# Two graph-attention layers on one core: a lighter feature, norm and score-offset path, and another order of steps on all five engines

## The chip, the cores and the metric

The kernel runs on one core of one Trainium2 chip. The metric is the device time of one execution in microseconds (us). TensorE is called PE below, VectorE DVE, ScalarE ACT, GpSimd POOL and SyncE SP; SP only issues DMAs here.

## What is computed

There are 64 graphs of 128 nodes with 384 features. Each passes a dot-product attention layer with 6 heads, a residual and a layer norm, then an additive attention layer with 12 heads, an elu, a sigmoid gate and a second layer norm. All of it is float32.

```python
q, k, v = heads(x @ Wq + bq), heads(x @ Wk + bk), heads(x @ Wv + bv)
probs = softmax(q @ k.T / sqrt(64) + where(adj, 0, -9e15))
x = layernorm(x + (probs @ v) @ Wf + bf)
h = einsum('bnd,ade->bane', x, W);  th = tanh(h)
attn = leaky_relu(th @ w_src + swap(th @ w_dst), 0.2)
attn = softmax(where(adj, attn, -999))
feat = elu(attn @ h + b)
gate = sigmoid(x @ H_w.T + H_b)
x = layernorm(x + gate * feat + (1 - gate) * x)
```

## The kernel before

Work goes by pairs of graphs (g is 0 or 1 in a pair), 32 pairs in all. The kernel is a software pipeline: in turn t of the loop, stage 0 handles the first layer of pair t, stage 1 the projections and scores of the second layer of pair t-1, and stage 2 the second attention product and the output of pair t-2. Stage -1 loads the next pair. A step called with `turn.late(s, ...)` in an engine's turn t belongs to the turn before, so it handles pair t-1-s, and a step called with `turn.step(s, ...)` handles pair t-s. Every engine runs its own list of steps strictly in the order written at the end of its block, and waits on semaphores (`now(...)`, `prev(...)`) for what other engines make. The lists of the five engines need not turn over at the same moment: an engine may be in its turn t+1 while PE is in turn t.

float32 products are made from rounded parts. A linear product takes three matmul passes (`product`, high and low parts), so ACT writes the high part of each operand and DVE the low part. The values `v` and the features `h` are cut in three bfloat16 parts: ACT writes parts 1 and 2, POOL makes the residue (`value_residue`, `hidden_residue`) and part 3 (`value_part3`, `hidden_part3`). `attend0(g)` on PE waits for `v_done[2][g]`, which is `value_part3(g)` on POOL.

For one pair the path around the change is this. `source_target_transposes` (line 502) turns the small score parts of the second layer, ACT copies them (`source_target_copy`, line 762), and `targets_flat` on SP issues six small DMAs (line 398) that lay them out in rows, which `attention1(g)` (lines 586 and 590) reads. The adjacency of a pair is loaded twice: `load_adj0` (line 381) for the first layer, where POOL makes `mask0` from it (`mask0_bias`, line 1238) for `scores(g)`, and `load_adj1` (line 387) for the second. `load_transposed_x` (line 369) brings the next pair's transposed input, from which ACT makes `xt_hi` (`next_x_high`). On SP the order before is:

```python
turn.late(0, load_adj1)
turn.late(-1, load_x)
turn.step(-1, load_transposed_x)
turn.step(1, targets_flat)
turn.step(-1, load_adj0)
turn.late(2, store, 0)
turn.late(2, store, 1)
```

On POOL, `mask0_bias` of pair t stands behind `value_residue(0)` of the same pair, and `value_part3(1)` of pair t comes in the same turn. PSUM banks are shared by rotation: `TP_USERS` and `LIN_USERS` name the users in PE's order, and the next user of a bank waits for the last reader of the one before.

Of the kernel before, what the change touches and what calls it, by code (L numbers as in the profile page):

```python
# [17 lines left out]
H0 = 6  # L18
E0 = D // H0
H1 = 12  # L20
# [3 lines left out]
MASKED = 9e15 / SCALE0  # L24
# [78 lines left out]
def turns(eng, passed, body, prepare=None):  # L103
# [10 lines left out]
    for t in range(PAIRS - 1, PAIRS + 3):  # L114
# [5 lines left out]
TP_USERS = ("ct1", "wt00", "wt01", "wt02", "x1t0", "wt10", "x1t1", "wt11", "wt12", "pt01", "sdt", "pt00",  # L120
             "pt11", "pt10", "ct0")
# [4 lines left out]
LATE_USERS = ("g1", "z1", "ct1", "pr0", "pr1")  # L126
# [19 lines left out]
def two_layer_graph_attention(nc, x, x_t, adj, weights, biases, row_biases, out):  # L146
    with ExitStack() as ctx:
# [20 lines left out]
        half_neg = sb("half_neg", [128, 1])  # L168

# [19 lines left out]
        p0_max = sb("p0_max", [128, 2, H0])  # L189
        p0_shift = sb("p0_shift", [128, 2, H0])  # L190
# [57 lines left out]
        bv_ready = signal("bv_ready", 0, 1)  # L248
        bv_mm = signal("bv_mm", 0, 1)
        bias_row_loaded = signal("bias_row_loaded", 0, 1)  # L250
        bias_split = signal("bias_split", 0, 1)
        bias_loaded = signal("bias_loaded", 0, 1)
# [17 lines left out]
        sc_mm, sc_max = pair_of("sc_mm", 0), pair_of("sc_max", 0)  # L270
        sc_shift, sc_exp = pair_of("sc_shift", 0), pair_of("sc_exp", 0)
# [29 lines left out]
        f_bias, f_min, f_exp = pair_of("f_bias", 2), pair_of("f_min", 2), pair_of("f_exp", 2)  # L301
# [41 lines left out]
        def _(sp):  # L343
# [18 lines left out]
            def body(turn):  # L362
# [58 lines left out]
        def _(pe):  # L421
# [16 lines left out]
            def body(turn):  # L438
# [180 lines left out]

                turn.late(1, gate_rows, 1)  # L620
# [7 lines left out]
                turn.step(0, queries_keys, 1)  # L628
                turn.step(2, attend1, 0, 0)
                turn.step(2, weights1_transposes, 0, 2)  # L630
                turn.step(0, values, 0)
                turn.step(2, attend1, 0, 1)
                turn.step(1, x1_transposes, 0)
                turn.step(0, queries_keys, 2)
                turn.step(2, attend1, 0, 2)
                turn.step(1, hidden, 0)
                turn.step(2, weights1_transposes, 1, 0)
# [18 lines left out]
                turn.step(0, context_transposes, 0)  # L656
# [6 lines left out]
        def _(act):  # L663
            def weight_high(n):
                act.wait_ge(w_loaded[n].sem, 16)
                act.activation(w_hi[n][:, :, :].rearrange("p c d -> p (c d)"), staging[n], ACT.Copy)\
                    .then_inc(w_hi_ready[n].sem, 1)
# [5 lines left out]
            def other_weights():  # L673
                act.wait_ge(small_loaded.sem, 16 * SMALL)

                act.activation(x1t_hi[:, 0, :, :], column["bv"][:, :].unsqueeze(2).to_broadcast([128, C, N]),
                               ACT.Copy).then_inc(bv_ready.sem, 1)
                for n in ("Wf", "W1", "Hw"):
                    weight_high(n)
# [7 lines left out]
            def body(turn):  # L687
# [18 lines left out]
                def keep_x1(g):  # L706
                    act.wait_ge(x1_ready[g].sem, prev(x1_ready[g]))

                    act.wait_ge(y2_ready[g].sem, now(y2_ready[g]))
                    act.activation(x1_kept[:, g, :], x1[:, g, :], ACT.Copy).then_inc(x1_copied[g].sem, 1)  # L710
# [7 lines left out]
                def hidden_part1(g):  # L718

                    act.wait_ge(f_mm[g].sem, now(f_mm[g]))  # L720
                    act.activation(h_part[0][:, g, :, 0:E1],
                                   lin_bank(f"h{g}")[:, 0:D].rearrange("p (a e) -> p a e", a=H1),
                                   ACT.Copy).then_inc(h_done[0][g].sem, 1)

                def hidden_copy(g):
                    act.wait_ge(h_mm[g].sem, now(h_mm[g]))

                    act.wait_ge(h_done[2][g].sem, prev(h_done[2][g]))
                    act.activation(h_res[:, g, :], lin_bank(f"h{g}")[:, 0:D], ACT.Copy).then_inc(h_raw[g].sem, 1)
# [49 lines left out]
                def scores_exp(g):  # L779
                    act.wait_ge(sc_shift[g].sem, now(sc_shift[g]))  # L780
# [3 lines left out]
                    for h in range(H0):  # L784
                        last = act.activation(p0[:, g, N * h:N * (h + 1)], zp[:, h // C, N * (h % C):N * (h % C + 1)],  # L785
                                              ACT.Exp, bias=p0_shift[:, g, h:h + 1], scale=SCALE0)
# [39 lines left out]

                def elu_exp(g):
# [581 lines left out]
```

## Time and profile before

| | |
|---|---|
| median of 3 runs | 1347.98 us (1346.89 to 1348.66) |
| the profiled execution, its own time | 1350.65 us |
| its span, first to last instruction | 1348.9 us |
| PE busy | 1200.5 us, 89% |
| DVE busy | 1077.4 us, 80% |
| POOL busy | 1006.0 us, 75% |
| ACT busy | 990.9 us, 73% |

The span is compared with the profiled execution's own time; the median of other executions is 2.67 us below that. Matmuls overlap, so a busy share of PE counts a little more than its rate; idle time is the surer sign.

### The profile page before, as it was taken

Reading aid. Unit: us, or ns where it says so; the run is one execution under the profiler, and the core shown is the slowest. Engines: PE = TensorE matmul, PEld = TensorE weight load, DVE = VectorE, ACT = ScalarE, POOL = GpSimd, SP = SyncE. Lnnn points to the kernel's source line nnn. Section 1 sums busy time; section 2 is a strip of 40 time slices with the busy share of each in tenths; the row PEclk is TensorE's granted clock in tenths of the full one; section 3 lists DMA queues with packets and bytes.
Section 4 is the critical chain, followed back from the end, with each engine's and each line's share of the span. In section 5 each row is a group of like instructions: output and inputs, shape, how many; then the busy total and the mean of one; then the engine's idle time right before and its main releaser. Section 6 shows DMA issues by size and latency. Waiting matters only on the chain.

```text
span 1348.9 us, 37937 instructions
## 1 busy us (share of the span) xinstructions
PE 1200.5 (89%) x13193; PEld 1066.4 (79%) x13193; DVE 1077.4 (80%) x2138; ACT 990.9 (73%) x2058; POOL 1006.0 (75%) x941
## 2 busy tenths in 40 slices
PE   4899999999999999999999999999999999999963
PEld 4788788888878888878888887888887888887752
DVE  5478788888888888888888888888888888888864
ACT  4377777777777777777777777777778778777753
POOL 1257877778887777887777788777788777878766
PEclk9799999999999999999999999999999999999976
DMA  3100010111010111101011100011110101110000
GB/s 130 50 27 28 16 39 25 37 37 37 14 37 24 37 37 38 37 14 37 24 37 37 37 19 33 25 36 37 37 37 14 37 24 37 37 37 26 15 13 24
DMA packets 46172, 44.86 MB, mean 33 GB/s; under 512 B 24757, under 2 KB 41146, under 8 KB 46138
## 3 DMA queue, kind: packets, MB, share of 16 engines
q1 hardware_dynamic: 46138, 44.42, 10.1%
q8 instruction: 20, 0.33, 0.1%
q14 instruction: 14, 0.11, 0.0%
HBM read 31.22 MB, written 12.58 MB: 32 GB/s over the span
## 4 chain that ended last, share of the span: by engine, by line
PE 53%; POOL 13%; issue 12%; DVE 10%; ACT 9%; DMA 1%; SPq 0%; DVEq 0%; POOLq 0%; ACTq 0%
PE lin L427 31%; PE tp L600 5%; DVE z L1084 4%; ACT p L785 3%; POOL f L1306 3%; PE zp L528 2%; POOL y L1331 2%; PE tp L565 2%; POOL v_res L1274 2%; PE zp L586 2%; PE fp L612 2%; POOL v_part L1278 2%; PE fp L553 2%; PE zp L590 2%; POOL rstd L1295 1%
## 5 line engine op out<-in xcount | busy, mean ns | idle before, releaser
L1300 POOL TENSOR_TENSOR z<-z,z_max 128x1536 f32<-128x1536 f32 x64 | 176.3, 2755 | 18.0 <-DVE z_max L1091 18.0
L1291 POOL TENSOR_TENSOR rstd<-rstd,half_neg 128x1 f32<-128x1 f32 x64 | 35.2, 549 | 163.3 <-DVE rstd L1071 163.3
L1253 POOL TENSOR_TENSOR prod<-th,w_sd_rows 128x768 f32<-128x768 f32 x64 | 120.1, 1876 | 36.0 <-ACT th L716 36.0
L824 ACT ACTIVATE p1t_hi<-tp 128x512 f16<-128x512 f32 x192 | 110.6, 593 | 37.6 <-PE tp L600 37.6
L1099 DVE SCALAR_TENSOR_TENSOR p1t_lo<-tp,p1t_hi 128x512 f16<-128x512 f32 x192 | 129.4, 688 | 8.0 <-ACT p1t_hi L824 5.0
L612 PE MATMUL fp<-h_part,p1t_hi 128*128 128x33 bf16 x2304 | 115.6, 179 | 4.5 <-DVE p1t_lo L1099 4.4
L612 PEld LDWEIGHTS fp<-h_part,p1t_hi 128*128 128x128 f16 x2304 | 102.5, 97 | 18.4 <-issue 12.7
L600 PE MATMUL tp<-ident,z 128*128 128x128 f32 x768 | 109.5, 280 | 7.4 <-ACT z L819 5.9
L1084 DVE SCALAR_TENSOR_TENSOR z<-zp,z 128x1536 f32<-128x1536 f32 x64 | 111.8, 1748 | 3.2 <-ACT z L794 3.2
L1091 DVE TENSOR_REDUCE z_max<-z 128x12 f32<-128x1536 f32 x64 | 111.3, 1738 | 0.1
L785 ACT ACTIVATE p<-zp,p_shift 128x128 f32<-128x128 f32 x384 | 105.6, 382 | 5.9 <-DVE p_shift L1022 5.9
L615 PE MATMUL fp<-h_part,p1t_lo 128*128 128x33 bf16 x1536 | 109.6, 178 | 0.0
L819 ACT ACTIVATE z<-z 128x1536 f32<-128x1536 f32 x64 | 95.3, 1488 | 13.8 <-POOL z L1300 13.8
L427 PE MATMUL lin<-xt_hi,Wq_hi 128*128 128x256 f32 x288 | 86.6, 301 | 18.4 <-POOL xt_lo L1283 18.0
L600 PEld LDWEIGHTS tp<-ident,z 128*128 128x128 f32 x768 | 90.5, 144 | 10.9 <-ACT z L819 6.7
L794 ACT ACTIVATE z<-zp 128x1536 f32<-128x1536 f32 x64 | 92.9, 1451 | 2.1 <-PE zp L590 2.1
L615 PEld LDWEIGHTS fp<-h_part,p1t_lo 128*128 128x128 f16 x1536 | 93.2, 96 | 0.0
L1331 POOL TENSOR_TENSOR y<-f,x_kept 128x384 f32<-128x384 f32 x64 | 64.8, 1013 | 34.7 <-ACT out_tile L835 29.6
L1313 POOL TENSOR_SCALAR f_neg<-f 128x384 f32<-128x384 f32 x64 | 74.8, 1168 | 12.8 <-POOL f L1306 11.9
L427 PE MATMUL lin<-xt_lo,Wq_hi 128*128 128x256 f32 x288 | 81.3, 282 | 0.0
L427 PE MATMUL lin<-xt_hi,Wq_lo 128*128 128x256 f32 x288 | 81.1, 282 | 0.0
L427 PE MATMUL lin<-xt_hi,Wk_hi 128*128 128x256 f32 x288 | 80.9, 281 | 0.0
(163 smaller groups left out, 4805.3 us busy)
## 6 DMA issues: line engine op xcount, KB each, us to landing
xt_raw<-x_t SPq DMA_DIRECT2D x32, 384.0 KB, 3.6
x_raw<-x SPq DMA_DIRECT2D x32, 384.0 KB, 3.1
out<-out_tile SPq DMA_DIRECT2D x64, 192.0 KB, 1.9
dst_row<-sd_t SPq DMA_DIRECT2D x192, 3.0 KB
adj<-adj SPq DMA_DIRECT2D x64, 32.0 KB, 1.9
z<-Wq SPq DMA_DIRECT2D x1, 576.0 KB, 3.6
z<-Wk SPq DMA_DIRECT2D x1, 576.0 KB, 4.6
p<-Wv SPq DMA_DIRECT2D x1, 576.0 KB, 6.6
```

What stands on the lines that cost most here:

```text
L427: last = pe.matmul(bank, a(k), b(k), start=(opens and k == 0 and i == 0), stop=(k == C - 1 and i == 2))
L600: last = pe.transpose(bank[:, N * i:N * (i + 1)], z[:, g, c:c + N], ident[:, :])
L612: pe.matmul(o, hi, h_part[i][:, g, h, :], start=(h == 0 and i == 0), stop=False, skip_group_check=True)
L615: last = pe.matmul(o, lo, h_part[i][:, g, h, :], start=False, stop=(i == 1), skip_group_check=True)
L785: last = act.activation(p0[:, g, N * h:N * (h + 1)], zp[:, h // C, N * (h % C):N * (h % C + 1)], ACT.Exp, bias=p0_shift[:, g, h:h + 1], sc ...
L819: act.activation(z[:, g, :], z[:, g, :], ACT.Exp).then_inc(z_exp[g].sem, 1)
L824: act.activation(p1t_hi[:, g, 4 * N * k:4 * N * (k + 1)], tp_bank(f"wt{g}{k}")[:, :], ACT.Copy, scale=PSCALE).then_inc(wt_hi[k][g].sem, 1)
L1084: dve.scalar_tensor_tensor(out=z[:, g, :], in0=zp[:, :, :].rearrange("p b n -> p (b n)"), scalar=0.2, in1=z[:, g, :], op0=ALU.mult, op1=AL ...
L1091: dve.tensor_reduce(z_max[:, g, :], z[:, g, :].rearrange("p (a n) -> p a n", a=H1), AX.X, ALU.max).then_inc(z_maxed[g].sem, 1)
L1099: dve.scalar_tensor_tensor(out=p1t_lo[:, g, c], in0=bank[:, :], scalar=PSCALE, in1=p1t_hi[:, g, c], op0=ALU.mult, op1=ALU.subtract)\
L1253: pool.tensor_tensor(prod[:, g, :].rearrange("p (s d) -> p s d", s=2), th[:, g:g + 1, :].to_broadcast([128, 2, D]), rows["w_sd"][:, :].rea ...
L1300: pool.tensor_tensor(zs, zs, z_max[:, g, :].unsqueeze(2).to_broadcast([128, H1, N]), ALU.subtract)\
```

## The change

Five things are altered.

- Features: b1 is added to the features `h` before they are cut in parts, on DVE while it copies them out of PSUM (`hidden_raised`, in place of ACT's `hidden_copy`). The stored b1 is raised by 1, so the attention output arrives as f+1. POOL's `features_bias` and its minimum are gone; ACT computes relu(1-(f+1)) and then exp of its negative, and DVE takes a plain maximum. `x1_kept` is also raised by 1, which cancels in the difference.
- Norms: the shift of each layer norm is a `tensor_scalar` with one tensor input instead of a `scalar_tensor_tensor` with two.
- Score offset: Wq and bq carry the factor and a minus sign, so DVE's minimum serves directly as the bias of the exponential and `scores_shift` is gone.
- The four small steps on the score parts handle both graphs in one instruction each instead of one per graph.
- The order of steps is another on PE, ACT, DVE, POOL and SP, with the bank rotation to match.

```diff
-TP_USERS = ("ct1", "wt00", ..., "pt11", "pt10", "ct0")
+TP_USERS = ("ct0", "ct1", "wt00", ..., "pt11", "pt10")
...
 # SP
-                turn.late(0, load_adj1)
-                turn.late(-1, load_x)
-                turn.step(-1, load_transposed_x)
+                turn.late(2, store, 0)
                 turn.step(1, targets_flat)
                 turn.step(-1, load_adj0)
-                turn.late(2, store, 0)
+                turn.step(-1, load_transposed_x)
+                turn.step(0, load_adj1)
                 turn.late(2, store, 1)
+                turn.late(-1, load_x)
...
 # PE
+                turn.late(0, context_transposes, 0)
                 turn.late(1, gate_rows, 1)
                 turn.late(1, attention1, 1)
                 turn.late(0, context_transposes, 1)
...
                 turn.step(1, attention1, 0)
-                turn.step(0, context_transposes, 0)
                 turn.step(0, attend0, 1)
...
 # ACT
+                def features_negative(g):
+                    act.wait_ge(f_norm[g].sem, now(f_norm[g]))
+                    act.wait_ge(f_elu[g].sem, prev(f_elu[g]))
+                    act.activation(f_neg[:, g, :], f[:, g, :], ACT.Relu, bias=one[:, :], scale=-1.0)\
+                        .then_inc(f_min[g].sem, 1)
...
                 turn.step(1, gate_tanh, 0)
                 turn.step(1, z_copy, 0)
                 turn.step(-1, next_x_high)
-                turn.step(1, hidden_part2, 0)
-                turn.step(1, hidden_part2, 1)
                 turn.step(0, context_high, 0)
-                turn.step(1, gate_quarter, 0)
-                turn.step(1, keep_x1, 0)
+                turn.late(2, norm1, 1)
+                turn.step(1, gate_tanh, 1)
+                turn.step(0, context_high, 1)
...
 # DVE
+                def hidden_raised(g):
+                    dve.wait_ge(h_tanh[g].sem, now(h_tanh[g]))
+                    dve.wait_ge(h_done[2][g].sem, prev(h_done[2][g]))
+                    dve.tensor_tensor(h_res[:, g, :].rearrange("p (a e) -> p a e", a=H1),
+                                      lin_bank(f"h{g}")[:, 0:D].rearrange("p (a e) -> p a e", a=H1),
+                                      rows["b1"][:, :].unsqueeze(1).to_broadcast([128, H1, E1]), ALU.add)\
+                        .then_inc(h_raw[g].sem, 1)
...
-                    dve.scalar_tensor_tensor(out=shift0[:, g, :], in0=moments[:, g, 0:1], scalar=-1.0,
-                                             in1=rstd[:, g, :], op0=ALU.mult, op1=ALU.mult)\
+                    dve.tensor_scalar(shift0[:, g, :], moments[:, g, 0:1], rstd[:, g, :], -1.0, ALU.mult, ALU.mult)\
...
+                turn.late(0, weights0_low, 1, 1)
+                turn.late(2, variance1, 0)
+                turn.late(2, elu, 1)
                 turn.late(0, context_inverse, 1)
-                turn.late(2, variance1, 0)
+                turn.late(1, z_leak, 0)
                 turn.late(0, context_norm, 1)
-                turn.late(1, z_leak, 0)
...
 # POOL: the whole new order
+                turn.late(1, hidden_residue, 0)
+                turn.late(2, gated_features, 0)
+                turn.late(0, value_part3, 0)
+                turn.late(2, mix, 0)
+                turn.late(0, value_residue, 1)
+                turn.step(0, mask0_bias)
+                turn.late(0, value_part3, 1)
+                turn.late(1, hidden_residue, 1)
+                turn.late(2, deviation1, 0)
+                turn.late(2, features_difference, 1)
+                turn.late(2, gated_features, 1)
+                turn.late(-1, next_x_low)
+                turn.late(1, z_subtract, 0)
+                turn.step(1, mask1_bias)
+                turn.late(2, mix, 1)
+                turn.late(1, hidden_part3, 0)
+                turn.late(0, deviation0, 0)
+                turn.late(1, z_subtract, 1)
+                turn.late(0, deviation0, 1)
+                turn.late(1, hidden_part3, 1)
+                turn.step(0, value_residue, 0)
+                turn.step(1, source_target_products, 0)
+                turn.step(1, source_target_products, 1)
+                turn.late(2, deviation1, 1)
+                turn.step(2, features_difference, 0)
```

## Rows read from the trace of the kernel before

**Rows 1.** Stretches: busy time of each engine and count, granted clock, DMA, one steady turn.
```profile
core 0: us, PE busy (x) PEld busy (x) DVE busy (x) ACT busy (x) POOL busy (x), PEclk, DMA share, GB/s
...
600.00:640.00 40.00, 37.10 (x416) 33.09 (x415) 33.27 (x68) 30.76 (x66) 31.63 (x30) 1.00 0.10 32
```

**Rows 2.** Who waited for whom: us in total, times, longest us.
```profile
PE tp L565 <- DVE p0t_lo L1030: 38.6, 30, 1.4
```

**Rows 3.** Timeline of PE: start us, us, what, idle before it and its releaser.
```profile
630.36 0.28 PE L502 MATMUL tp<-ident_bf,sd_parts 128*128 128x128 bf16 x2 [0.42 <-DVE sd_parts L990]
...
632.98 0.25 PE L553 MATMUL fp<-v_part,p0t_hi 128*128 128x65 bf16 x3 [0.27 <-POOL v_part L1278]
...
635.54 0.81 PE L590 MATMUL zp<-dst_row,sd_t 128*128 128x512 bf16 x3
637.71 0.52 PE L565 MATMUL tp<-ident,ctx_n 128*128 128x128 f32 x3 [1.35 <-DVE p0t_lo L1030]
638.17 0.25 PE L553 MATMUL fp<-v_part,p0t_hi 128*128 128x65 bf16 x3
...
641.78 0.39 PE L586 MATMUL zp<-mask,ident_bf 128*128 128x512 bf16 x1 [0.76 <-DVE z L1084]
...
670.12 0.28 PE L502 MATMUL tp<-ident_bf,sd_parts 128*128 128x128 bf16 x2 [0.41 <-DVE sd_parts L990]
```

**Rows 4.** Timeline of SP, the same turn.
```profile
631.59 4.74 SPq L398 DMA_DIRECT2D dst_row<-sd_t  x6
636.61 0.39 SPq L381 DMA_DIRECT2D adj<-adj  x1
637.37 0.98 SPq L405 DMA_DIRECT2D out<-out_tile  x2
```

**Rows 5.** Line 381, the load of the adjacency.
```profile
DMA to landing us min/median/max: 1.7/1.8/6.8
```

**Rows 6.** Timeline of POOL, the same turn.
```profile
619.04 0.40 POOL L1238 TENSOR_SCALAR mask<-adj 128x256 bf16<-128x256 uint8 x1
619.52 1.01 POOL L1306 TENSOR_TENSOR f<-f,b_rows 128x384 f32<-128x384 f32 x1
...
631.99 0.89 POOL L1278 TENSOR_TENSOR v_part<-v_res,v_part 128x384 bf16<-128x384 f32 x1
```

**Rows 7.** Groups of the page: the instructions that the feature edit removes or resembles.
```profile
L1313 POOL TENSOR_SCALAR f_neg<-f 128x384 f32<-128x384 f32 x64 | 74.8, 1168 | 12.8 <-POOL f L1306 11.9
L1306 POOL TENSOR_TENSOR f<-f,b_rows 128x384 f32<-128x384 f32 x64 | 64.3, 1005 | 7.9 <-DVE f L1112 5.5
L829 ACT ACTIVATE f_neg<-f_neg 128x384 f32<-128x384 f32 x64 | 34.3, 536 | 39.2 <-POOL f_neg L1313 39.2
```

**Rows 8.** Lines 1078 and 1134: ns min/median/max, first and last start.
```profile
L1078 DVE SCALAR_TENSOR_TENSOR shift<-moments,rstd x64: 95/598/2230, 61.0 to 1293.5; 128x1 f32<-128x1 f32 x64
...
L1134 DVE TENSOR_SCALAR rstd<-moments x64: 113/144/155, 122.6 to 1344.4; 128x1 f32<-128x1 f32 x64
```

**Rows 9.** Timeline of PE where its granted clock is low, and after.
```profile
1287.24 0.25 PE L612 MATMUL fp<-h_part,p1t_hi 128*128 128x33 bf16 x3 [1.90 <-DVE p1t_lo L1099]
...
1307.48 0.36 PE L502 MATMUL tp<-ident_bf,sd_parts 128*128 128x128 bf16 x2 [3.41 <-DVE sd_parts L990]
1307.63 0.53 PE L471 MATMUL lin<-bias_rows,ones_bf 128*128 128x384 bf16 x1
...
1310.52 0.52 PE L427 MATMUL lin<-Hw_hi,x1t_lo 128*128 128x384 f32 x1
...
1312.79 0.34 PE L471 MATMUL lin<-bias_rows,ones_bf 128*128 128x384 bf16 x1 [0.22 <-ACT gate L770]
...
1314.36 0.34 PE L427 MATMUL lin<-Hw_hi,x1t_lo 128*128 128x384 f32 x1
```

**Rows 10.** Stretches with low clock (columns as in rows 1).
```profile
1287.50:1297.00 9.50, 7.07 (x76) 6.33 (x73) 5.71 (x13) 3.85 (x6) 6.40 (x6) 0.50 0.01 2
...
1307.70:1310.90 3.20, 3.20 (x13) 2.89 (x11) 0.95 (x4) 0.91 (x2) 2.85 (x4) 0.50 0.02 5
```

More of the change, by code:

```diff
@@ L635, in body @@
                 turn.step(2, attend1, 0, 2)
+                turn.step(2, weights1_transposes, 1, 0)
                 turn.step(1, hidden, 0)
-                turn.step(2, weights1_transposes, 1, 0)
                 turn.step(1, x1_transposes, 1)
@@ L876, in body @@
                 turn.step(0, scores_exp, 0)
+                turn.step(1, hidden_part1, 0)
                 turn.step(0, value_part1, 1)
+                turn.step(0, weights0_high, 0, 1)
                 turn.step(0, value_copy, 1)
-                turn.step(0, weights0_high, 0, 1)
                 turn.step(1, hidden_part1, 1)
-                turn.step(1, hidden_copy, 1)
                 turn.late(2, norm1, 0)
@@ L884, in body @@
                 turn.step(0, weights0_high, 0, 0)
+                turn.step(0, scores_exp, 1)
+                turn.step(2, features_negative, 1)
                 turn.step(0, value_part2, 1)
-                turn.step(0, scores_exp, 1)
-                turn.step(2, elu_exp, 1)
                 turn.step(0, weights0_high, 1, 1)
                 turn.step(0, weights0_high, 1, 0)
-                turn.late(2, norm1, 1)
+                turn.step(2, elu_exp, 1)
                 turn.step(1, gate_tanh, 0)
@@ L1158, in body @@
                 turn.late(0, variance0, 0)
+                turn.late(2, stats1, 1)
                 turn.step(2, weights1_low, 0, 0)
[L1160 removed]
                 turn.step(2, weights1_low, 0, 1)
                 turn.late(0, shift_norm0, 0)
+                turn.step(0, queries_keys, 0)
+                turn.late(0, stats0, 1)
+                turn.late(2, moments1, 1)
                 turn.step(0, queries_keys, 1)
[L1164 to L1166 removed]
                 turn.late(0, moments0, 1)
@@ L1170, in body @@
                 turn.step(1, x1_low, 0)
-                turn.late(2, variance1, 1)
-                turn.step(2, features_inverse, 0)
-                turn.late(0, shift_norm0, 1)
-                turn.step(2, features_norm, 0)
-                turn.step(0, queries_keys, 2)
-                turn.step(1, x1_low, 1)
+                turn.late(0, shift_norm0, 1)
+                turn.step(2, features_inverse, 0)
+                turn.step(0, queries_keys, 2)
+                turn.step(2, features_norm, 0)
+                turn.step(1, x1_low, 1)
+                turn.late(2, variance1, 1)
                 turn.step(2, weights1_low, 1, 0)
-                turn.step(0, scores_max, 0)
+                turn.step(0, scores_min, 0)
+                turn.step(1, hidden_raised, 0)
                 turn.step(2, elu, 0)
-                turn.step(0, scores_shift, 0)
                 turn.step(1, source_target_sums, 0)
```

175 lines of the change are left out of this document (68 added, 107 removed).

## The prediction

> **What bounds the kernel now.** I read the stretches first. In a steady stretch of 40 us PE is busy 37.10, DVE 33.27, POOL 31.63, ACT 30.76 [rows 1]. PE is the bound, and what is left to gain lies in its waits. The timeline of PE gives the length of a turn: the small transposes of line 502 start at 630.36 and again at 670.12, so a turn lasts 39.76 us [rows 3]. In this turn PE waits 0.42 us for the score parts, 0.27 for POOL's third value part, 1.35 for DVE's `p0t_lo` ahead of the context transposes of line 565, and 0.76 for `z` [rows 3]; a further 0.3 or so lies in overlaps lost at these points. The list of waits confirms that the third is a steady one: 30 times, 38.6 us in all [rows 2]. If every wait went, a turn would be near 37, the busy time. That is the most that a new order can give: about 2.8 us a turn, 85 to 90 us in all.
>
> **The lighter work.** POOL loses line 1306 (1.005 us) and line 1313 (1.168 us), twice a turn: 4.35 us of 31.6 [rows 7]. ACT gains a relu twice a turn; the trace has none, the nearest row is the exponential of the same shape, 0.536 us [rows 7], and it loses as many copies of that size (`hidden_copy`): about zero, between -0.5 and +0.5 us a turn. DVE gains `hidden_raised` (two additions of about the size of a 128x384 operation, some 0.55 us each), and loses `scores_shift` and half of the small score instructions. Its norm offsets are the interesting part: the two-input form of line 1078 has a median of 598 ns and up to 2230 for one element a partition, while the one-input form of line 1134 on the same shape never takes more than 155 [rows 8]. If the new offsets behave like line 1134, the first of them alone saves DVE around 0.45 us twice a turn by the medians; at worst they stay as they are, nothing. All of this shortens engines that are not the bound. I cost it at nothing in the steady turn, because PE's remaining work covers it: DVE and POOL have 6 to 8 us of slack a turn. Where that cover is absent, in the drain after the last pair has left PE's dense part, the feature path is shorter by 1.005 + 1.168 - 0.536 = 1.64 us per graph; with two graphs partly overlapped, and less queueing on POOL, I take 4 us, from bounds 0 and 8.
>
> **The new order, step by step.** On PE, `context_transposes(0)` leaves its place ahead of `attend0(1)` and goes behind it, so `attend0(1)` now stands directly behind `attention1(0)`. With DVE's `weights0_low` and ACT's `weights0_high` brought forward, that takes away most of the 1.35 us wait, if `attend0(1)` gets its other input in time. That input is `value_part3(1)` from POOL, and here I find the trouble. It must be followed through three queues.
>
> POOL's turn t+1 now begins with the late steps of turn t, and in their middle stands `turn.step(0, mask0_bias)`. As a `step` it belongs to pair t+1. Behind it in the queue is `late value_part3(1)`, of pair t, which PE wants for `attend0(1)` in its turn t. `mask0_bias` waits for the adjacency of pair t+1. SP issues that load in its turn t, behind `targets_flat`, and `targets_flat` waits for the score copy of PE's turn t, that is, for line 502 near the turn's end. Before, SP had the same order of these two, but POOL asked for the mask early in the next turn, at 619.04 against a load issued at 636.61 less one turn, 596.9, and nothing waited [rows 4, 6]. Now a chain closes inside one turn:
>
> - from line 502 on PE to the first flat DMA: 631.59 - 630.36 = 1.23 us [rows 3, 4];
> - the six issues on SP: 4.74 us [rows 4];
> - to the issue of `load_adj0`: 636.61 - 636.33 = 0.28 us [rows 4];
> - its landing: 1.8 us, least 1.7 [rows 5];
> - `mask0_bias` to the next instruction of POOL: 619.52 - 619.04 = 0.48 us [rows 6];
> - `value_part3(1)` and the hand-over to PE: 632.98 - 631.99 = 0.99 us [rows 3, 6].
>
> The sum is 9.5 us from line 502 to the start of `attend0(1)`. Before, it was 638.17 - 630.36 = 7.81 us [rows 3].
>
> The rest of the turn, from `attend0(1)` to the next line 502, was 39.76 - 7.81 = 31.95 us. Out of it I take both waits in it, 0.76 and 0.42, since the new orders bring `z_leak` and the score parts forward and the stall in front gives DVE and ACT time to catch up; the moved transposes come in, 638.17 - 637.71 = 0.46. That is 31.23 us. The new turn is 31.2 + 9.5 = 40.8 us after rounding up a little for hand-overs, 1.0 longer than before. If one of the two waits stays it is 41.5.
>
> Who stands behind the stalled instruction: on POOL `value_part3(1)`, `hidden_residue(1)`, the features of graph 1 and `next_x_low`; on PE everything. The moves on SP make two more loads late. `load_transposed_x` now follows `load_adj0`, and ACT's `next_x_high` waits for it with `context_high(0)`, `norm1(1)` and `gate_tanh(1)` behind it; and `load_x` goes behind a store that waits for that `norm1(1)`. By the same rows both arrive 1 to 7 us after `attend0(1)` starts, about when PE's own steps need them. I cost these at nothing, at most 0.5 us a turn; their cover is the stall itself.
>
> **The clock.** The stall is long for PE. In the chain, the last matmuls ahead of it (line 590) start 5.18 us after line 502 at the distance of before (635.54 - 630.36) and run 0.81 [rows 3], so PE then stands idle 9.5 - 6.0 = 3.5 us each turn. Where PE had stood idle 3.41 us, its clock was granted at 0.50 from then on (1.2 GHz) for some 3 us, and after 1.90 us idle near 1287 it stayed there for the 9.5 us shown [rows 9, 10]; the waits of 1.35 us in the steady turns leave it at 1.00 [rows 1, 3]. So I expect the low level after most stalls. Its price: the ten matmuls of a gate product take 1310.52 - 1307.63 = 2.89 us between first and last start at the low level and 1314.36 - 1312.79 = 1.57 at the high one [rows 9], so 46% of low time is lost. For a stretch of 3.2 us, as in the second row [rows 10], that is 1.5 us; for one of 9.5 us, 4.4; and 0 if the clock holds. I take 1.5, as PE's work is dense behind this stall, like behind the one of 3.41 us. The Trainium skill (TensorE: Matmul & The Clock Gate, section The HAM clock gate) says that an idle stretch puts the engine back to half its clock and that sustained work releases it; by that rule the turn is 42.3 us, and if 3.5 us idle were still short enough for it, 40.8. By that rule, the trace agrees: it fell after 3.41 us idle.
>
> **Sum.** The load of pair t+1 exists for t up to 30, and `targets_flat` has work from turn 1, so 30 turns carry the chain: 30 x (1.0 + 1.5) = 75 us. Turn 31 has no next mask and keeps the good of the new order, -3; the drain -4; the first two turns, whose line 502 to `attend0(1)` was shorter than later, +1. From the profiled execution: 1350.65 + 75 - 6 = 1419.7. The median of the runs lies 2.67 below it: 1417.
>
> **Rivals.**
>
> The order works (other side). If the mask's input were there when POOL comes to it, `attend0(1)` would start about 5.4 us after line 502 (7.81 less 1.35, 0.46, 0.27 and some lost overlap), and a turn would cost PE's own work, about 37 us: 32 x 2.8 = 90 less, and 4 in the drain: 1254. It decides at one point: the chain from line 502 to the end of `mask0_bias` would have to take under 4.4 us, and the six issues alone take 4.74 [rows 4]. For it speak the idle list of PE and the lighter POOL. 0.12, mostly for an error of mine in the turn to which a step belongs.
>
> The chain holds but the clock doesn't fall: 30 x 1.0 - 6 = +24, 1372. The stall would be interrupted or shortened, for instance by line 590 itself waiting for its DMAs. 0.2.
>
> The chain, and long low stretches: 30 x (1.0 + 4.4) - 6 = +156, 1504. Against it speaks the dense work behind the stall. 0.1.
>
> The edits cancel: the six issues turn out shorter, or more of the old waits goes than I counted, and a turn stays at 39.8: 1344 with the drain's gain. 0.06.
>
> **Numbers.** My forecast, chain and one low stretch a turn, has 0.52. Its own range is 1390 to 1455, from 0.7 to 1.9 us for clock and old waits around the 2.5. The 8-in-10 range takes in the rival without a clock drop and leaves out the two far ones: 1363 to 1460. A measurement of this kernel tells about 0.2% from no change. Slower by more than that: 0.52 + 0.2 + 0.1 and a part of the wash, 0.84; faster 0.13; the same 0.03.
>
> **What would show it.** In the profile after: PE's largest idle before line 553 of `attend0(1)`, released by POOL's `v_part`, near 3.5 us a turn; on POOL an idle gap before `mask`, ended by the DMA of `adj`; a turn of 42.3 us between two starts of line 502, 9.5 of it to `attend0(1)`; granted clock near 0.95 on average in steady turns instead of 1.00; the wait of line 565 for `p0t_lo` gone; the norm offsets at some 150 ns. Wrong would be: a turn of 37 us with no wait for the mask (then I have misread the queues), or the stall there with the clock at 1.00 (then only the last term falls).

## The result and the profile after

The changed kernel takes 1461.35 us (median of four executions) against 1348.32 us (1346.89 to 1348.87) for the kernel before: 1.083 times as long, interval 1.0807 to 1.0854. Three of the four took 1457.42 to 1461.69 us; the fourth took 1940.06 us in a slow state, at a mean granted clock of 0.557, and is left out of the ratio. The profiled execution has an own time of 1461.69 us, a span of 1460.0 us and a mean granted clock of 0.921. The sign and the chain behind it were forecast, 1417 us was 44 us too low, and the time lies 1.35 us above the top of the range.

A long stretch of steady turns of the changed kernel (columns as in [rows 1]):

```profile
600.00:1000.00 400.00, 354.82 (x3762) 320.52 (x3760) 285.01 (x567) 280.07 (x589) 240.63 (x226) 0.93 0.10 28
```

PE is busy 35.5 us in 40 here, 37.1 before [rows 1], although part of the 35.5 runs at half clock and is thereby longer. The clock is 0.93 where it was 1.00. No engine has become the bound; PE waits. The list of waits over the whole span (us in total, times, longest) says for what:

```profile
POOL mask L1243 <- DMA adj<-adj: 178.2, 27, 6.8
...
PE fp L553 <- POOL v_part L1283: 110.8, 30, 4.3
ACT xt_hi L849 <- DMA xt_raw<-x_t: 77.8, 30, 3.3
```

The first two lines are the forecast chain: POOL waits for an adjacency that wasn't waited for before, and PE for the value part queued behind that mask. The wait of line 565 for `p0t_lo` [rows 2] is gone. One turn on PE, the counterpart of [rows 3] (in other turns the wait of line 553 is up to 4.3 us, 3.7 on average):

```profile
643.09 0.28 PE L502 MATMUL tp<-ident_bf,sd_parts 128*128 128x128 bf16 x2 [0.87 <-DVE sd_parts L1004]
643.64 0.52 PE L538 MATMUL tp<-ident,p 128*128 128x128 f32 x3 [0.27 <-DVE p0t_lo L1038]
...
647.99 0.81 PE L590 MATMUL zp<-dst_row,sd_t 128*128 128x512 bf16 x3
652.91 0.33 PE L553 MATMUL fp<-v_part,p0t_hi 128*128 128x65 bf16 x3 [4.12 <-POOL v_part L1283]
...
658.42 0.95 PE L586 MATMUL zp<-mask,ident_bf 128*128 128x512 bf16 x3
```

From line 502 to `attend0(1)` it is 652.91 - 643.09 = 9.82 us (forecast: 9.5). Line 586 no longer waits for `z` (0.76 before). But line 502 still waits for the score parts, and longer: 0.87 us where [rows 3] had 0.42. Line 502 starts at 74.9 the first time and at 1422.2 the last, 31 turns apart, so the mean turn is 1347.3 / 31 = 43.46 us; worked out in the same way it was 1230.6 / 31 = 39.70 before. All "mean turns" below are of this kind. The last of the 31 is short, 35.1 us, since no next pair is loaded in it; the 30 that carry the chain take 43.74 on average, against 39.65 before. Of these 30, 25 take 43.2 to 44.4 us and 5 take 41.4 to 42.7. One of each kind, columns as in [rows 1]:

```profile
643.09:687.34 44.25, 38.99 (x412) 35.25 (x413) 31.30 (x63) 30.62 (x64) 26.65 (x26) 0.92 0.10 29
731.57:774.31 42.74, 37.63 (x412) 34.12 (x413) 31.31 (x63) 30.68 (x64) 26.65 (x26) 0.96 0.11 30
```

The work is the same; the granted clock is 0.92 in the 25 longer turns and 0.96 in the 5 shorter ones, so the low level lasts about twice as long in most turns as in the few short ones.

The chain on SP and POOL, against [rows 4, 6]:

```profile
644.22 4.67 SPq L398 DMA_DIRECT2D dst_row<-sd_t  x6
649.36 0.39 SPq L381 DMA_DIRECT2D adj<-adj  x1
650.05 0.35 SPq L369 DMA_DIRECT2D xt_raw<-x_t  x1
```

```profile
643.88 0.89 POOL L1279 TENSOR_TENSOR v_res<-v_res,v_part 128x384 f32<-128x384 f32 x1
651.44 0.40 POOL L1243 TENSOR_SCALAR mask<-adj 128x256 bf16<-128x256 uint8 x1 [6.67 <-DMA adj<-adj]
651.93 0.89 POOL L1283 TENSOR_TENSOR v_part<-v_res,v_part 128x384 bf16<-128x384 f32 x1
```

Line 381 is issued 6.27 us after line 502 starts; the mask starts 2.08 us later and `v_part` 0.49 after that; 0.98 us more and PE goes on. Two stretches behind the stall show the price in clock:

```profile
653.00:660.00 7.00, 7.00 (x51) 5.89 (x51) 4.44 (x5) 2.42 (x4) 5.64 (x6) 0.59 0.27 82
660.00:666.00 6.00, 6.00 (x44) 5.83 (x42) 4.28 (x6) 4.49 (x6) 4.33 (x4) 1.00 0.01 2
```

PE is busy without a gap from 653 to 660, at a granted clock of 0.59 on average, that is, mostly at the lower of its two levels, 1.2 GHz.

The norm offsets became cheap, though not as cheap as the 150 ns of the forecast: line 1086 takes 204 ns in the median (202 to 214), where the old form took 598 and up to 2230 [rows 8].

The growing wait at line 502 needs VectorE and GpSimd side by side. The four steps that make the score parts, on DVE in the changed kernel:

```profile
640.03 0.33 DVE L991 CAST sd_parts<-sd 128x48 bf16<-128x48 f32 x1 [0.20 <-DVE sd L982]
...
640.87 0.36 DVE L995 TENSOR_TENSOR sd_res<-sd,sd_parts 128x48 f32<-128x48 f32 x1
641.33 0.84 DVE L1000 CAST sd_parts<-sd_res 128x48 bf16<-128x48 f32 x1
642.27 0.76 DVE L1004 TENSOR_TENSOR sd_parts<-sd_res,sd_parts 128x48 bf16<-128x48 f32 x1
```

and GpSimd at the same time:

```profile
640.28 0.88 POOL L1267 TENSOR_TENSOR h_res<-h_res,h_part 128x384 f32<-128x384 f32 x1
641.12 1.00 POOL L1316 TENSOR_TENSOR f<-f,gate 128x384 f32<-128x384 f32 x1
642.09 0.88 POOL L1283 TENSOR_TENSOR v_part<-v_res,v_part 128x384 bf16<-128x384 f32 x1
```

The last three small operations end at 641.23, 642.17 and 643.03, and the GpSimd operations at 641.16, 642.12 and 642.97: each within 0.07 us behind the other. The kernel before, in the same place of a turn, on DVE:

```profile
667.97 1.07 DVE L978 TENSOR_TENSOR sd_res<-sd,sd_parts 128x24 f32<-128x24 f32 x2
669.07 0.26 DVE L984 CAST sd_parts<-sd_res 128x24 bf16<-128x24 f32 x2
...
669.80 0.26 DVE L990 TENSOR_TENSOR sd_parts<-sd_res,sd_parts 128x24 bf16<-128x24 f32 x2
```

and on POOL:

```profile
667.91 1.00 POOL L1323 TENSOR_TENSOR f<-f,gate 128x384 f32<-128x384 f32 x1
669.89 1.03 POOL L1331 TENSOR_TENSOR y<-f,x_kept 128x384 f32<-128x384 f32 x1 [0.99 <-ACT out_tile L835]
```

There the pair of line 978, started under a GpSimd operation, took 1.07 us, and the pair of line 984, in GpSimd's gap, 0.26. It looks as if a small operation sits on DVE until GpSimd's is over. That is so far a reading; e6 below tests it.

### The profile page after: what moved, and what is told of

It is laid out like the page before. It is cut to its first block, busy times and chain, and to the rows that moved or that the text cites. A ratio compares the mean times of both kernels' runs of the same rounds, so it can differ in the third digit from the quotient of the medians.

```text
span 1460.0 us, 37822 instructions
## 1 busy us (share of the span) xinstructions
PE 1257.6 (86%) x13193; PEld 1133.9 (78%) x13193; DVE 1022.5 (70%) x2011; ACT 994.6 (68%) x2060; POOL 856.1 (59%) x813
## 4 chain that ended last, share of the span: by engine, by line
issue 26%; PE 22%; POOL 21%; DVE 14%; SPq 9%; DMA 4%; ACT 2%; POOLq 0%; DVEq 0%; ACTq 0%
PE lin L427 11%; SPq L398 8%; POOL prod L1258 8%; POOL z L1305 5%; DMA adj<-adj 3%; PE fp L553 2%; DVE z L1091 2%; PE tp L565 2%; POOL rstd L1296 2%; DVE sd L982 2%; POOL v_res L1279 2%; DVE y L1066 2%; POOL v_part L1283 2%; DVE sd_parts L1000 2%; PE zp L586 2%
## 5 line engine op out<-in xcount | busy, mean ns | idle before, releaser
L553 PE MATMUL fp<-v_part,p0t_hi 128*128 128x65 bf16 x1152 | 82.6, 213 | 113.5 <-POOL v_part L1283 110.8
L553 PEld LDWEIGHTS fp<-v_part,p0t_hi 128*128 128x128 f16 x1152 | 70.6, 110 | 133.7 <-issue 133.7
L1045 DVE RECIPROCAL ctx_rcp<-fp 128x6 f32<-128x6 f32 x64 | 12.5, 196 | 180.7 <-PE fp L556 180.7
L1243 POOL TENSOR_SCALAR mask<-adj 128x256 bf16<-128x256 uint8 x32 | 13.4, 417 | 214.3 <-DMA adj<-adj 178.2
L1106 DVE SCALAR_TENSOR_TENSOR p1t_lo<-tp,p1t_hi 128x512 f16<-128x512 f32 x192 | 126.0, 683 | 3.6 <-ACT p1t_hi L821 3.5
L612 PE MATMUL fp<-h_part,p1t_hi 128*128 128x33 bf16 x2304 | 111.6, 178 | 1.2 <-DVE p1t_lo L1106 1.2
L782 ACT ACTIVATE p<-zp,p_min 128x128 f32<-128x128 f32 x384 | 105.9, 388 | 5.6 <-DVE p_min L1030 5.6
L1296 POOL TENSOR_TENSOR rstd<-rstd,half_neg 128x1 f32<-128x1 f32 x64 | 35.1, 549 | 117.1 <-DVE rstd L1079 117.1
L427 PE MATMUL lin<-Hw_hi,x1t_hi 128*128 128x384 f32 x192 | 95.6, 498 | 0.0
```

What stands on the lines that cost most here:

```text
L427: last = pe.matmul(bank, a(k), b(k), start=(opens and k == 0 and i == 0), stop=(k == C - 1 and i == 2))
L553: pe.matmul(o, hi, v_part[i][:, g, head, :], start=(h == 0 and i == 0), stop=False, skip_group_check=True)
L612: pe.matmul(o, hi, h_part[i][:, g, h, :], start=(h == 0 and i == 0), stop=False, skip_group_check=True)
L1106: dve.scalar_tensor_tensor(out=p1t_lo[:, g, c], in0=bank[:, :], scalar=PSCALE, in1=p1t_hi[:, g, c], op0=ALU.mult, op1=ALU.subtract)\
```

## The experiments

All times below are medians, of two executions in e2, e3 and e5 and of four to ten in the others; each ratio is to the kernel before as measured beside that run (1348.37 to 1349.39 us). Unless something else is said, each kernel is the changed one with the edit shown.

**e1, the adjacency ahead of the targets' copies.**

```
 turn.late(2, store, 0)
+turn.step(-1, load_adj0)
 turn.step(1, targets_flat)
-turn.step(-1, load_adj0)
```

> The changed kernel with one step moved on SP: load_adj0 ahead of targets_flat. Theory (the mask's load behind the six flat issues holds POOL's third value part, and PE with it): the wait of line 553 for POOL's v_part goes, and with it the low clock. The transposed input still loads behind the flat issues, about 9.7 us after line 502, so ACT's xt_hi waits and with it the context's high part; PE would wait some 1.5 us for that. A turn of 38 to 39.5 us instead of 44.25, in all 1265 to 1310 us. Rival (the new order of PE, ACT and DVE is itself worse, and the mask only one of several waits): a turn stays above 42 us, over 1390 us.

1356.33 us, 1.0049 of before (1.0023 to 1.0076), mean turn 40.11. The edit of one line gives back 105 of the 113 us, so the loss hangs on the chain through SP. POOL no longer waits for the adjacency beyond 0.5 us and PE's 4.12 us are 0.28. The level was missed by 46 us, since two loads are still late:

```profile
DVE y L1066 <- DMA x_raw<-x: 52.0, 27, 2.3
...
ACT xt_hi L849 <- DMA xt_raw<-x_t: 50.8, 30, 2.6
```

and PE now feels it:

```profile
653.64 0.35 PE L427 MATMUL lin<-xt_hi,Wq_hi 128*128 128x256 f32 x1 [0.77 <-DVE y L1066]
```

**e2, adjacency and transposed x ahead of the targets' copies.**

```
 turn.late(2, store, 0)
+turn.step(-1, load_adj0)
+turn.step(-1, load_transposed_x)
 turn.step(1, targets_flat)
-turn.step(-1, load_adj0)
-turn.step(-1, load_transposed_x)
```

> The changed kernel with load_adj0 and load_transposed_x both ahead of targets_flat on SP. Theory: nothing of stage -1 is late any more; a turn of 36.8 to 38 us, near PE's own work, in all 1230 to 1275 us, and 20 to 50 us less than with load_adj0 alone. Rival (the transposed input's lateness costs nothing, as the prediction had it): the same time as with load_adj0 alone, within 10 us.

1309.91 us, 0.9703 of before (0.9672 to 0.9734): mean turn 38.63, 46 us below e1, inside the 20 to 50 expected, and faster than the kernel before, but 35 us above the level expected. What was left:

```profile
693.49 0.28 PE L502 MATMUL tp<-ident_bf,sd_parts 128*128 128x128 bf16 x2 [0.88 <-DVE sd_parts L1004]
```

```profile
655.40:661.40 6.00, 5.49 (x58) 4.10 (x59) 4.39 (x12) 5.19 (x15) 3.83 (x5) 1.00 0.37 106
...
694.70:697.90 3.20, 3.20 (x22) 2.89 (x21) 1.19 (x4) 2.85 (x9) 1.13 (x3) 0.52 0.45 131
```

The same wait at line 502 as in the changed kernel is there in every turn (655.42, 693.49, 733.12). Behind the one at 655.42 the clock stays at 1.00 and the turn takes 38.07 us; behind the one at 693.49 it is 0.52 for 3.2 us and the turn takes 39.63. Each time PE waits 0.88 us and, at line 538, 0.27 us more; behind it the clock falls in 8 of the 28 turns that have these two waits, each time for 1.5 us more, and in the other 20 it doesn't.

**e3, the mask behind the last value part on POOL**, SP's order left as in the changed kernel.

```
+turn.late(0, value_part3, 1)
 turn.step(0, mask0_bias)
-turn.late(0, value_part3, 1)
```

> The changed kernel, SP's order untouched, with mask0_bias and late value_part3(1) swapped on POOL, so that the third value part no longer stands behind the mask. Theory: attend0(1) starts some 5 to 6 us after line 502 instead of 9.8 and the clock stays up; POOL still idles for the mask until some 8.5 us after line 502, so next_x_low and the features behind it are late, and PE waits 1 to 3 us for xt_lo or xt_hi instead: a turn of 38.5 to 41 us, in all 1280 to 1360 us. Rival (what holds PE is that POOL as a whole is late, whatever stands behind the mask): the turn stays within 1 us of 44.25.

1380.78 us, 1.0228 (1.0184 to 1.0272), mean turn 40.82: the turn is inside the 38.5 to 41 expected, the time 21 us above the 1360 expected at most. The chain can be cut on POOL as well as on SP: PE waits 0.28 us at `attend0(1)`, released by DVE. The loads stay late, ACT's copy of x_t waits 86.4 us in all (77.8 before this edit), and PE waits 0.85 us for `y` and 0.66 for `ctx_lo`. So it is worth 24 us less than e1. The clock stays up as expected: it falls in 1 of the 28 turns in which PE, here too, waits 0.89 us at line 502 and 0.27 at line 538.

**e4, the kernel before with the changed kernel's order of SP's steps**, and nothing else.

```
-turn.late(0, load_adj1)
-turn.late(-1, load_x)
-turn.step(-1, load_transposed_x)
+turn.late(2, store, 0)
 turn.step(1, targets_flat)
 turn.step(-1, load_adj0)
-turn.late(2, store, 0)
+turn.step(-1, load_transposed_x)
+turn.step(0, load_adj1)
 turn.late(2, store, 1)
+turn.late(-1, load_x)
```

> The kernel before with only the changed kernel's order of SP's steps (store, targets, first adjacency, transposed x, second adjacency, store, x); every other engine keeps its order. My theory: the order of SP's loads costs what it does only together with GpSimd's new place for the mask, ahead of the last value part; in the old GpSimd order the mask reads an adjacency that was loaded some 20 us earlier. The transposed x is now issued about 28 us later, right behind the adjacency (676.8 in the turn at 671), and lands some 3.4 us after, while ScalarE copied it at 678.7: up to 1.8 us of wait on ScalarE in a turn, most of it absorbed. Expected 1345 to 1385 us, no wait of TensorE on the value parts. Rival: SP's order is harmful by itself, whatever GpSimd does: 1420 us or more.

1360.26 us, 1.0087 (1.0064 to 1.011). SP's order costs 11 us by itself (ACT stands idle for 1.21 us ahead of its copy of x_t in a turn) and not 113: the loss needs both, loads behind the copies and the mask ahead of the value part.

**e5, PE kept busy in the stall.** Sixteen matmuls of 128x512 more a turn ahead of `attend0(1)`, whose results nothing reads:

```
+if g == 1:
+    for _ in range(16):
+        pe.matmul(fp[:, 0:512], ones_bf, ident_bf (repeated), start=True, stop=True)
 pe.wait_ge(v_done[2][g].sem, now(v_done[2][g]))
```

> The changed kernel, with 16 extra matmuls of 512 columns whose result is overwritten, placed on PE in the stall ahead of the wait for POOL's v_part in attend0(1), so that PE has work while it stalls. The stall itself stays. Theory (the low clock after the stall costs 2.3 us a turn): the granted clock stays at 1.00 in the steady turns and a turn falls from 44.25 to about 41.9 us, in all 1385 to 1400 us. Rival (the slower matmuls lie beside other waits and cost little): the clock stays up and the time falls by less than 20 us.

1409.45 us, 1.044 (1.0404 to 1.0476), mean turn 41.75:

```profile
600.00:1000.00 400.00, 384.89 (x4127) 335.31 (x4126) 299.34 (x600) 295.21 (x622) 255.69 (x239) 0.99 0.10 29
```

More work on PE, and 52 us less time. The chain is as it was, POOL waits 178.3 us for the adjacency against 178.2, and the clock is at 0.99. The low clock therefore costs at least 52 us of the changed kernel's time, (43.46 - 41.75) = 1.7 us a turn. That is less than the 2.3 us that I expected, and the time is 9 us above the 1400 expected at most. It is a lower bound for two reasons: 8 of the first 30 turns are still at 0.96, and the last turn, which has no stall for the sixteen matmuls to fill, went from 35.1 to 39.6 us. The 22 turns at a clock of 1.00 take 41.58 us on average, against the 43.74 of the changed kernel: about 2.2 us a turn that carries the chain.

**e6, e2 with GpSimd idle while the score parts are made.** A wait more on POOL, behind the two products:

```
+def hold():
+    pool.wait_ge(sd_3.sem, now(sd_3))
 ...
 turn.late(2, deviation1, 1)
+turn.step(1, hold)
 turn.step(2, features_difference, 0)
```

> The kernel with the first adjacency and the transposed x ahead of the targets (1309.91 us), and GpSimd now waits, behind the two products, until VectorE has written the third score part. There VectorE's four small operations took 0.33, 0.36, 0.84 and 0.76 us, each of the last three ending within 0.06 us of the end of a GpSimd operation; TensorE waited 0.88 us at L502 in every turn, and in every second turn a stretch of half clock followed (turns of 38.1 and 39.6 us). Theory: VectorE's operations that read two tensors or a tensor in SBUF are held by a running GpSimd operation; with GpSimd idle each takes under 0.25 us, the wait at L502 is under 0.2 us, the low stretches behind it go too, and the turn is 37.2 to 37.6 us: 1255 to 1280 us. Rival: the small operations are slow because they are merged (48 elements in three dimensions), so the wait at L502 stays at 0.7 us or more: 1305 us or more, longer still for GpSimd's lost time. Second rival: the wait goes, and GpSimd's 2 us later value parts make TensorE wait at the context product instead: 1290 to 1330 us.

1301.06 us, 0.9636 (0.9617 to 0.9655); mean turn 38.34. Line 502 doesn't wait any more in the steady turns (3.0 us in two waits at the start, 32.0 in 32 waits in e2), and 29 of the first 30 turns are at a clock of 1.00. The four operations, still merged and with nothing of them changed, take 0.19 to 0.21 us each with GpSimd idle, the last two a quarter of their time (shown from e12, which has the same wait):

```profile
640.87 0.19 DVE L991 CAST sd_parts<-sd 128x48 bf16<-128x48 f32 x1 [0.20 <-DVE sd L982]
...
641.61 0.20 DVE L995 TENSOR_TENSOR sd_res<-sd,sd_parts 128x48 f32<-128x48 f32 x1
641.91 0.19 DVE L1000 CAST sd_parts<-sd_res 128x48 bf16<-128x48 f32 x1
642.20 0.21 DVE L1004 TENSOR_TENSOR sd_parts<-sd_res,sd_parts 128x48 bf16<-128x48 f32 x1
```

The merging is thereby excluded as the cause, and it is shown that these operations are held while GpSimd works. But the time fell by 9 us and not by 30 to 55; the second rival is what came: GpSimd's 2.5 us are missing further on.

```profile
651.56 0.25 PE L553 MATMUL fp<-v_part,p0t_hi 128*128 128x65 bf16 x3 [1.12 <-POOL v_part L1283]
```

**e7, the changed kernel's operations in the old orders.** All lighter operations, every engine's steps and PSUM banks as before.

```
 turn.step(0, scores_min, 0)
+turn.step(1, hidden_raised, 0)
 ...
+turn.step(2, features_negative, 0)
 turn.step(2, elu_exp, 0)
```

> The changed kernel's operations (one addition less and no minimum on GpSimd, relu on ScalarE, the bias added to the hidden values on VectorE, minimum of negative scores, merged score parts, new offsets) in the old order on every engine and with the old banks; only the steps that are new stand beside their neighbours (the relu ahead of the exponential, the raised values behind the minimum of the scores and behind the shift of the second norm). Theory: the lighter work lies off the path that sets the turn, so the time is that of the kernel before within 15 us: 1333 to 1363 us, and all of the loss of 113 us is the order's. Rival: the lighter work is what would have paid and gives 20 us or more by itself: 1325 us or less. Second rival: the operations themselves cost, since VectorE has an addition of 0.55 us more for each graph where ScalarE had a copy: 1370 us or more.

1344.45 us, 0.9966 (0.9957 to 0.9976). The lighter work is worth 4.6 us, about what the forecast gave to the drain, and all of the loss is the order's. The first 30 turns take 39.69 us on average, 39.65 before. This kernel also settles where the growth at line 502 comes from: with the merged operations in the old order PE waits 17.8 us there in all (18.3 before, 31.8 in the changed kernel), and the last two of them take 0.19 and 0.20 us, both started in a gap of 1.02 us in GpSimd's work.

**e8, the kernel before with e6's wait.**

```
 turn.step(1, source_target_products, 1)
+turn.step(1, hold)
```

> The kernel before with one wait more: GpSimd waits behind the two products until VectorE has written the third score part. VectorE's residues there took 1.07 us for two while a GpSimd operation ran, and its other small operations 0.13 us each. Theory: TensorE's wait of 0.42 us at L502 goes or nearly goes, and GpSimd, which was idle for 1.0 us in that stretch anyway, is 1 to 2 us later with the minimum that ScalarE's exponential waits for: 1335 to 1365 us. Rival: the later minimum holds ScalarE's copies of the weights behind it, which TensorE waits for at the context product: 1365 us or more.

1413.42 us, 1.0477 (1.0458 to 1.0496): far worse, and my theory wrong, the rival right in size but with another place. In the old order POOL makes graph 0's last value part behind the gated features, the mask and the mix, all of which the wait delays; PE then stands still at `attend0(0)`, for which the profile names no releaser:

```profile
655.03 0.28 PE L502 MATMUL tp<-ident_bf,sd_parts 128*128 128x128 bf16 x2
660.15 0.25 PE L553 MATMUL fp<-v_part,p0t_hi 128*128 128x65 bf16 x3 [2.78 <-issue]
```

POOL writes that part at 659.17 for 0.88 us, and PE goes on at 660.15. 0.42 us were removed at line 502 and 2.78 put in 5 us later. The clock was 0.97 in the steady stretch.

**e9, e6 with graph 0's last value part between the two products.**

```
 turn.step(1, source_target_products, 0)
+turn.step(0, value_part3, 0)
 turn.step(1, source_target_products, 1)
 ...
-turn.late(0, value_part3, 0)
```

> The kernel in which GpSimd waits for the third score part (1301.06 us; turn 38.45), with one step moved: GpSimd writes graph 0's last value part (0.9 us) between the two products, where it waits 1.0 us for the second tanh, instead of behind the gated features. In the run with the wait alone, L502 no longer waited, and TensorE waited 1.12 us for that part ahead of the context product of graph 0. Theory: that wait was all that took the gain; it goes, 0.3 to 0.5 us at the context product of graph 1 stay, no low stretches of the clock: turn 37.2 to 37.6, 1255 to 1275 us. Rival: the part in the new place delays the second product and with it the score parts, so that L502 waits again: 1290 us or more.

1294.96 us, 0.9587 (0.956 to 0.9614), mean turn 38.13. Neither case came: no wait at line 502 nor at either `attend0`, and yet 6 us only, since the next input in line is the targets' copies:

```profile
651.35 0.59 PE L590 MATMUL zp<-dst_row,sd_t 128*128 128x512 bf16 x2 [1.44 <-DMA dst_row<-sd_t]
```

**e10, the changed kernel with e6's wait on POOL alone**, mask and SP's order untouched.

> The changed kernel, its order of SP's steps and its mask as they are, with GpSimd waiting behind the products for the third score part. The chain from L502 over the targets' copies, the adjacency, the mask and the last value part to the context product is left as it is; only its start, the score parts, comes earlier by the 0.87 us that TensorE waits for them now. Theory: the turn is that chain (9.8 us) and the rest, and each us by which its start comes earlier is a us off the turn: 32 x 0.87 = 28, 1425 to 1440 us; the wait of 4.1 us at L553 stays. Rival: the rest of the turn has another limit close behind, and the 0.87 us turn up in another wait: 1455 us or more. Second rival: a good part of the half-clock work came from the wait at L502, and goes too: 1420 us or less.

1420.32 us, 1.0538 (1.0504 to 1.0571), mean turn 42.14:

```profile
664.25 0.28 PE L502 MATMUL tp<-ident_bf,sd_parts 128*128 128x128 bf16 x2
667.69 0.25 PE L553 MATMUL fp<-v_part,p0t_hi 128*128 128x65 bf16 x3 [1.09 <-POOL v_part L1283]
...
673.90 0.25 PE L553 MATMUL fp<-v_part,p0t_hi 128*128 128x65 bf16 x3 [3.17 <-POOL v_part L1283]
```

The chain holds, 673.90 - 664.25 = 9.65 us, and the turn is 1.32 us shorter: the 0.87 us, and 0.45 more. The granted clock over the steady stretch went from 0.93 to 0.95 with it, and the turns are mixed: of the first 30, 4 are at a clock of 1.00 and take 40.75 us on average, 13 at 0.96 and 13 at 0.92. Against the 41.58 of e5 at that clock, 0.8 us went with the wait itself; the rest of the 41 us is low clock that went too. So the first theory has its 27 us and the second rival the remaining 14, on the border of what either expected. What the run does not separate: its stall also falls in two parts, 1.09 and 3.17 us, where it was one of 4.12.

**e11, e2 with the early value part and no wait.** Edit as in e9, on e2.

> The kernel with adjacency and transposed x first (1309.91 us) with graph 0's last value part between the two products, and no wait added on GpSimd. GpSimd goes on straight behind the products with other additions, so VectorE's residue and part operations stay held by them. Theory: the wait of 0.88 us at L502 stays, and so do the half-clock stretches in every second turn: 1300 to 1315 us. Rival: one GpSimd operation fewer behind the products lets VectorE through: L502 waits 0.2 us or less and the time is below 1285 us.

1301.81 us, 0.9637 (0.9608 to 0.9666), mean turn 38.33. The time is inside what the theory gave, but not for its reasons: the wait at line 502 fell to 0.47 us, the low stretches were gone (clock 1.00 in the steady stretch), and 0.71 us of waiting for the targets' copies had come.

**e12, e9 with the next pair's loads at the head of SP's turn.** In order: adjacency, transposed x, store of graph 0, targets, x, second adjacency, store of graph 1.

> The kernel with GpSimd's wait and the early value part (1294.96 us; turn 38.2) with one more order of SP's steps: adjacency and transposed x of the next pair at the head of the turn, ahead of the store of graph 0, then the targets' copies, x, the second adjacency, the store of graph 1. TensorE's one wait there is 1.44 us at L590 of graph 0 for the targets' copies, which are issued behind the store (0.36 us), the adjacency (0.39) and the transposed x (0.35), 2.2 us after the store's issue. The next pair's adjacency and transposed x can be loaded some 20 us earlier, since their tiles are free by then, so the copies start 1.3 to 1.5 us earlier. Theory: that wait falls to under 0.2 us and nothing takes its place: turn 36.8 to 37.1, 1246 to 1265 us. Rival: behind it stands the chain over the weights of graph 1 and the context products, and the turn stays above 37.7: 1280 us or more.

1289.45 us, 0.9556 (0.9543 to 0.9569), mean turn 37.97. The wait for the copies is gone, and the rival is right: behind it stood the weights of graph 1.

```profile
649.55 0.25 PE L553 MATMUL fp<-v_part,p0t_hi 128*128 128x65 bf16 x3 [1.30 <-DVE p0t_lo L1038]
```

On ACT, the copies that DVE needs for it stand behind a step that waits for GpSimd:

```profile
647.53 0.53 ACT L749 ACTIVATE v_part<-v_res 128x384 bf16<-128x384 f32 x1 [1.41 <-POOL v_res L1279]
647.96 0.85 ACT L797 ACTIVATE p0t_hi<-tp 128x384 f16<-128x384 f32 x2
```

This is the fastest kernel of the study, 60 us below the kernel before and 172 below the changed one. Swapping these two steps on ACT would be next; it wasn't tried.

## Why the prediction was right in kind and too low

**The turn to which a step belongs, and the chain: right.** The mask of the next pair stands ahead of this pair's last value part, its adjacency behind the six copies, and these behind line 502. It measured 9.82 us for a forecast 9.5, term by term: 6.27 to the issue of line 381 (6.25), 2.08 for the landing and POOL's start on it (1.8), 0.49 and 0.98 (0.48 and 0.99). The landing was short by 0.3. e1, e3 and e4 show that it is this chain and that it needs both orders.

**The clock: the fall was right, the size too small.** Forecast 1.5 us a turn, from one low stretch, and a clock near 0.95. e5 gives 1.7 by the mean turns and 2.2 by the turns that carry the chain, and the clock was 0.93, since most turns had about twice that low time. The rival without a clock fall would have needed that clock to hold.

**The step that failed: "I take both waits in it, 0.76 and 0.42, since the new orders bring `z_leak` and the score parts forward".** The 0.76 went. The 0.42 at line 502 stayed and grew to 0.87. The forecast turn was 42.3 us; the 30 turns that carry the chain measured 43.74, 1.4 more, which is 43 of the 44 us. Without low clock the forecast was 40.8, and e5's turns at a clock of 1.00 take 41.58: 0.8 more, with 0.87 for this wait, 0.3 for the chain and some 0.4 less elsewhere. The other 0.6 is clock, 2.2 for 1.5. The prediction had itself said "if one of the two waits stays it is 41.5" for the turn without the clock, but took the other value. e10 takes away the wait and leaves SP's order and the mask as they are: its turns at a clock of 1.00 take 40.75 us, its 30 turns 42.37, so that the clock costs 1.6, and it lands at 1420.32, 3 us from the forecast of 1417. With the wait, then, went both what it cost itself and most of the clock's excess.

I had treated the score parts as a question of their place in DVE's queue. They are a question of what GpSimd does meanwhile (e6, e7). Before, DVE's last two steps began in the gap that GpSimd spent waiting for `out_tile`. In the new order GpSimd has no gap there and goes from one addition to the next, and each of DVE's small steps is held for what is left of one of them. The Trainium skill (SBUF — State Buffer, section SBUF: two separate sides) says that VectorE and GpSimd share one port pair as an exclusive lock, which a VectorE operation needs in a 2-port mode or with two inputs in SBUF, and that whichever starts second is blocked for the other's whole instruction. The trace agrees: the last three small operations above end 0.05 to 0.07 us behind GpSimd's, and take 0.19 to 0.21 us with GpSimd idle.

**The range:** the upper end of the forecast's own range, 1455, doesn't follow from its terms. The chain's 1.0 us and the 1.9 given as the most for clock and old waits make 2.9 a turn and 1429 us. The measured turn grew by 4.1 us.

**Late loads at "nothing, at most 0.5 us a turn": right for this kernel only.** The stall covers them. With the stall gone, x_t alone was worth 46 us (e1 against e2), 1.5 us a turn.

**The lighter work at nothing in the turn, 4 us at the end: right.** e7 gives 4.6 us in all and nothing in the first 30 turns. In the changed kernel the time from the last line 502 to the end is 37.8 us, 41.4 before.

**The rival "the order works", 1254 us: no run came near it.** Its premise, the mask's input in time, is e2, and that stood at 1309.91. Even with four waits removed one after the other (e2, e6, e9, e12) the turn is 37.97 and not 37: each removal showed another wait, of 0.88, 1.12, 1.44 and 1.30 us. I had read "if every wait went" off PE's idle time, which tells what PE could gain if nothing stood behind its waits. The waits that a timeline shows are only those that come last.

What stays open: why the clock is low for about twice the time in most turns of the changed kernel and in fewer turns of e10. It goes with the wait at line 502 or with the stall's being in one piece; no run separates the two.

## What to carry to other kernels

When a step changes its place in a queue, write down which iteration it belongs to, and follow its input through every queue to where that input is issued: here one load behind six small issues and one mask ahead of a value part cost 113 us together, and with either of the two put right 8 or 32 were left (e1, e3). Keep loads that have no dependence on this iteration's work at the head of the issuing queue. Read a short operation's duration beside what the neighbouring engine does at the same time: if it ends when the other ends, its time isn't its own, and making the other engine denser will lengthen it. And cost a wait as gone only if its releaser's whole chain becomes shorter, not because its steps moved up.

## What the runs showed that I had not expected

VectorE's operations on 48 elements a partition with all operands in SBUF took 0.76 to 0.84 us while GpSimd ran its additions and 0.19 to 0.21 us with GpSimd idle, and the one-element offsets of the new form took 0.20 to 0.22 in both kernels. Sixteen matmuls a turn in PE's idle time, 512 columns each, made the changed kernel 52 us faster. A wait of 0.88 us at line 502, with 0.27 us of another close behind, was followed by some 3 us of half clock in 8 of 28 turns of e2, at 1.5 us a time, and by none in the other 20; in e3 the same two waits were followed by it in 1 turn of 28. The wait alone therefore doesn't decide it.
